# Counting pairs of nodes in one word: the first layer of a two-layer graph network on one core

## The reference

```python
def L0(edge_index, x):                       # the first layer: the change is here
    deg = segment_sum(ones, col)
    norm = deg_inv_sqrt[row] * deg_inv_sqrt[col]
    return segment_sum(x[row] * norm[:, None], col)

x = layernorm(x + L0(edge_index, x))
x = layernorm(x + L1(x, edge_index, edge_attr_4, edge_attr_32, W1, b1, W2, b2, si_w0, si_w1))
```

## Time and profile before

| | us |
|---|---|
| median of three runs | 3286.57 |
| profiled execution, its own time | 3279.85 |
| its span in the trace | 3278.0 |
| set-up, until the first gather | 82 |
| first layer, first gather to last table product | 82 to 1152 |
| second layer, from its first gather | 1171 to 3278 |

### The profile page before, as it was taken

The page is one execution under the profiler, slowest core; times in us unless marked ns, Lnnn a source line. Parts: engine busy times, 40 slices in busy tenths (PEclk is TensorE's granted clock), DMA queues, the critical chain, the costliest instruction groups (busy, mean ns, idle before and its releaser), DMA issues.

```text
span 3278.0 us, 48226 instructions
## 1 busy us (share of the span) xinstructions
PE 2556.6 (78%) x16782; PEld 1514.3 (46%) x16782; DVE 2876.8 (88%) x5078; ACT 1266.1 (39%) x1963; POOL 2400.0 (73%) x2477
## 2 busy tenths in 40 slices
PE   5798888898898867777777777777777777777776
PEld 4566666666676633333333333333343334333333
DVE  7787887787787759999999999999999999999998
ACT  2787887897888831111111111111111111111111
POOL 1777777777777757777777777777777777777775
PEclk7899999999999988998989999889889888888888
DMA  3111111111111121111111111111111111111112
GB/s 79 45 20 20 19 20 20 20 20 20 20 20 20 20 41 28 29 30 31 28 28 29 28 28 28 28 29 28 32 28 29 29 28 29 29 28 29 29 32 37
DMA packets 169490, 93.10 MB, mean 28 GB/s; under 512 B 112489, under 2 KB 155305, under 8 KB 169129
## 3 DMA queue, kind: packets, MB, share of 16 engines
q0 software_dynamic: 78336, 46.43, 10.6%
q1 hardware_dynamic: 90921, 43.61, 5.4%
HBM read 82.64 MB, written 7.22 MB: 27 GB/s over the span
## 4 chain that ended last, share of the span: by engine, by line
POOL 39%; DVE 23%; issue 17%; PE 14%; ACT 5%; DMA 1%; DVEq 1%; POOLq 0%; SPq 0%; ACTq 0%
POOL gathered L571 39%; DVE stage L1537 8%; PE ps L835 6%; PE ps L850 4%; DVE prod_all L1527 4%; ACT room L640 4%; DVE prod_all L1521 3%; DVE gathered L1209 2%; DVE stage L1511 1%; PE ps L775 1%; DVE stage L1507 1%; PE ps L742 1%; DVE prod_all L1343 1%; DMA gathered<-split_table,efT_all 1%; PE ps L822 1%
## 5 line engine op out<-in xcount | busy, mean ns | idle before, releaser
L571 POOL DMA_INDIRECT gathered<-x_table,idx x1664 | 1572.1, 945 | 533.0 <-issue 502.6
L571 POOL DMA_INDIRECT gathered<-split_table,efT_all x752 | 776.2, 1032 | 239.3 <-issue 232.9
L640 ACT ACTIVATE room<-ps 128x1089 bf16<-128x1089 f32 x800 | 877.7, 1206 | 181.1 <-PE ps L835 180.6
L955 PE MATMUL ps<-w2t,hT 128*128 128x512 f32 x1664 | 876.4, 653 | 16.3 <-ACT hT L691 16.2
L1537 DVE TENSOR_REDUCE stage<-prod_all 128x192 f32<-128x1536 f32 x416 | 725.3, 1744 | 3.2
L835 PE MATMUL ps<-prod_all,lane 128*128 128x363 bf16 x2640 | 571.1, 326 | 104.9 <-ACT room L640 54.5
L955 PEld LDWEIGHTS ps<-w2t,hT 128*128 128x128 f32 x1664 | 343.9, 213 | 373.3 <-issue 242.8
L943 PE MATMUL ps<-efT_all,w 128*128 128x512 f32 x416 | 270.2, 737 | 275.3 <-DMA sh<-in_sh 274.9
L850 PE MATMUL ps<-stage,room 128*128 128x96 bf16 x7840 | 474.4, 209 | 0.0
L850 PEld LDWEIGHTS ps<-stage,room 128*128 128x128 bf16 x7840 | 429.2, 100 | 82.5 <-issue 4.5
L699 ACT ACTIVATE stage<-gathered 128x64 f32<-128x64 f32 x416 | 105.1, 253 | 933.7 <-DMA gathered<-x_table,idx 933.7
(11 more groups left out here) (156 smaller groups left out, 1548.3 us busy)
## 6 DMA issues: line engine op xcount, KB each, us to landing
efT_all<-in_efT SPq DMA_DIRECT2D x104, 256.0 KB
gathered<-x_table,idx POOLq DMA_INDIRECT x1664, 2.4
gathered<-split_table,efT_all POOLq DMA_INDIRECT x752
sh<-in_sh SPq DMA_DIRECT2D x104, 32.0 KB
split_table<-stage SPq DMA_DIRECT2D x1, 2352.0 KB, 7.3
idx<-in_src SPq DMA_DIRECT2D x104, 8.0 KB, 1.6
scaled_x_table<-room SPq DMA_DIRECT2D x2, 784.0 KB, 3.4
x_table<-x_sb SPq DMA_DIRECT2D x7, 224.0 KB, 4.7
```

The source lines that it names most:

```text
L571: pool.indirect_dma_start(to, None, table, bass.IndirectOffsetOnAxis(ap=at, axis=0)).then_inc(landed, 16)
L640: act.activation(counts[u % 2][:, :, t * TWIN:(t + 1) * TWIN].rearrange("p (r h) w -> p r h w", r=RANGES), ps_ring[i % 2].rearrange("p r ( ...
L955: mm = pe.matmul(ps_bank[j % 2][v], hT[j // 2][:, t * P:(t + 1) * P], w2t[:].rearrange("p h c o i -> p (h c o i)"), start=False, stop=True)
```

## The change

Two neighbouring high parts h share one 32-bit word. The one-hot of the low part is no longer 1 but 1 or 65536, by the lowest bit of h, and `spread` is made of `11 (h/2) + target`: 550 columns instead of 1089. A count in PSUM is then `even + 65536 odd`; ACT writes it as an int32 word, and the two 16-bit halves of a word, read as fp16, are the two counts times 2^-24. `apply_counts` reads every second 16-bit element as its weights, and `take_rows` multiplies by 2^24. The ranges are two of 275 columns, two banks, and the ring has three entries in the same six banks. ACT copies all tiles; DVE copies none. The shares are new: 7 chunks and 16 units in a pattern, thus 38 gathered chunks (608 gathers) and 96 counted units (1056 tiles). The set-up computes the weight and the key of the pair in five more steps. Some small tiles moved into the room of a larger one.

```diff
-UPP = 8
-DVE_TILES = (5,)
-CPP = 5
+UPP = 16
+CPP = 7
 UW = 104
 D3 = 96
-RANGES = 3
-HR = 33
+RANGES = 2
+HR = 25
+RING = 3
+HALF = 2.0 ** 16
+HALF_ULP = 2.0 ** -24
...
-        ones_at = sb("ones_at", [P, 2 * CHUNKS], BF16)
+        ones_at = prod_all[:, 0].rearrange("p t c i o -> p (t c i o)")[:, DT:DT + CHUNKS].bitcast(BF16)
...
-        near_lanes = sb("near_lanes", [P, LW], F16)
-        low_lanes = sb("low_lanes", [P, 3, 44], F16)
+        near_lanes = sb("near_lanes", [P, 2 * WIDE], F16)
...
+        pos = flat[:, 3 * WIDE + DT:3 * WIDE + DT + U]
+        low_lanes = flat[:, 3 * WIDE - 66:3 * WIDE].bitcast(F16).rearrange("p (a b) -> p a b", b=44)
...
+        weight = flat[:, 3 * WIDE:3 * WIDE + DT]
...
-        counts = [t[:].bitcast(BF16).rearrange("p (h w) -> p h w", w=P) for t in room]
+        pair_words = [t[:].rearrange("p (h w) -> p h w", w=P) for t in room]
+        counts_i = [t[:].bitcast(I32).rearrange("p (h w) -> p h w", w=P) for t in room]
+        counts = [t[:].bitcast(F16).rearrange("p (h w v) -> p h w v", w=P, v=2) for t in room]
+        pair = dsrc.bitcast(F32)
...
-        ps_ring = [ps[:, RANGES * b:RANGES * (b + 1), 0:RW] for b in range(2)]
+        ps_ring = [ps[:, RANGES * b:RANGES * (b + 1), 0:RW] for b in range(RING)]
...
-                    act.wait_ge(s_evict, act_evicts(UT * (u - 1)))
+                    act.wait_ge(s_evict, UT * (u - 1))
                     act.wait_ge(s_apply, u - 1)
-                act.activation(counts[u % 2][:, :, t * TWIN:(t + 1) * TWIN].rearrange("p (r h) w -> p r h w", r=RANGES),
-                               ps_ring[i % 2].rearrange("p r (h w) -> p r h w", w=TWIN),
+                act.activation(counts_i[u % 2][:, :, t * TWIN:(t + 1) * TWIN].rearrange("p (r h) w -> p r h w", r=RANGES),
+                               ps_ring[i % RING].rearrange("p r (h w) -> p r h w", w=TWIN),
                                ACT.Copy).then_inc(s_evict, 1)
...
-                act.activation(rows_u[:], ps_dense, ACT.Copy).then_inc(s_dsb, 1)
+                act.activation(rows_u[:], ps_dense, ACT.Copy, scale=1.0 / HALF_ULP).then_inc(s_dsb, 1)
...
-                    if t not in DVE_TILES:
-                        evict(u, t)
+                    evict(u, t)
...
-                if i >= 2:
-                    if (i - 2) % UT in DVE_TILES:
-                        pe.wait_ge(s_evict_d, dve_evicts(i - 1))
-                    else:
-                        pe.wait_ge(s_evict, act_evicts(i - 1))
+                if i >= RING:
+                    pe.wait_ge(s_evict, i - RING + 1)
                 for r in range(RANGES):
-                    mm = pe.matmul(ps_ring[i % 2][:, r, :], ohlow[:, i % LR, 0:P], spread[i % KR][:, r * RW:(r + 1) * RW],
+                    mm = pe.matmul(ps_ring[i % RING][:, r, :], ohlow[:, i % LR, 0:P], spread[i % KR][:, r * RW:(r + 1) * RW],
                                    start=True, stop=True)
...
-                    pe.wait_ge(s_evict, act_evicts(UT * (u + 1)))
-                    pe.wait_ge(s_evict_d, dve_evicts(UT * (u + 1)))
+                    pe.wait_ge(s_evict, UT * (u + 1))
...
-                    mm = pe.matmul(ps_dense, counts[u % 2][:, h, :], table[:, h, :], start=(h == 0), stop=(h == NP - 1))
+                    mm = pe.matmul(ps_dense, counts[u % 2][:, h // 2, :, h % 2], table[:, h, :], start=(h == 0), stop=(h == NP - 1))
...
-            dve.wait_ge(s_key, 5)
-            for to, of, offset in zip(counted_places(key), counted_places(high), counted_tiles(rel_tile)):
+            dve.tensor_scalar(weight[:].bitcast(I32), dsrc, 7, 1, ALU.logical_shift_right,
+                              ALU.bitwise_and).then_inc(s_key, 1)
+            dve.wait_ge(s_key, 6)
+            dve.tensor_scalar(key[:].bitcast(I32), dsrc, 8, None, ALU.logical_shift_right).then_inc(s_key, 1)
+            dve.tensor_copy(weight[:], weight[:].bitcast(I32)).then_inc(s_key, 1)
+            dve.wait_ge(s_key, 8)
+            dve.tensor_copy(pair, key[:].bitcast(I32)).then_inc(s_key, 1)
+            dve.tensor_scalar(weight[:], weight[:], HALF - 1.0, 1.0, ALU.mult, ALU.add).then_inc(s_key, 1)
+            dve.wait_ge(s_key, 9)
+            for to, of, offset in zip(counted_places(key), counted_places(pair), counted_tiles(rel_tile)):
...
-                dve.tensor_scalar(ohlow[:, i % LR, 0:P + 1], low_lanes[:, :, 0:43], low[:, i:i + 1], None,
-                                  ALU.is_equal).then_inc(s_ohlow, 1)
-                dve.tensor_scalar(spread[i % KR], near_lanes[:], key[:, i:i + 1], None, ALU.is_equal).then_inc(s_spread, 1)
-
-            def evict(u, t):
-                i = u * UT + t
-                dve.wait_ge(s_count, i + 1)
-                if u >= 2:
-                    dve.wait_ge(s_apply, u - 1)
-                dve.tensor_copy(counts[u % 2][:, :, t * TWIN:(t + 1) * TWIN].rearrange("p (r h) w -> p r h w", r=RANGES),
-                                ps_ring[i % 2].rearrange("p r (h w) -> p r h w", w=TWIN)).then_inc(s_evict_d, 1)
+                dve.tensor_scalar(ohlow[:, i % LR, 0:P + 1], low_lanes[:, :, 0:43], low[:, i:i + 1], weight[:, i:i + 1],
+                                  ALU.is_equal, ALU.mult).then_inc(s_ohlow, 1)
+                dve.tensor_scalar(spread[i % KR], near_lanes[:, 0:LW], key[:, i:i + 1], None, ALU.is_equal).then_inc(s_spread, 1)
...
-                        made = u * UT + t - (KR - 1)
-                        if 0 <= made < DT and made % UT in DVE_TILES:
-                            evict(made // UT, made % UT)
```

More of the change, by code:

```diff
@@ L76, in gnn_program @@
     RW = HR * TWIN
-    LW = -(-RANGES * RW // 4) * 4
+    WORDS = RANGES * HR
+    LW = -(-WORDS * TWIN // 4) * 4
     RISE = n_out / CHUNKS
@@ L85, in gnn_program @@
     assert CHUNKS % 2 == 0 and CHUNKS >= 8 and n_out + UW <= SUMW and NP % SPLITS == 0
-    assert NP % HB == 0 and (RANGES - 1) * HR < NP <= RANGES * HR and RW <= WIDE and CHUNKS % 4 == 0 and NP % GB == 0
-    assert CG * TPC + DT == TILES and CG % 2 == 1 and UT * TWIN <= P and DT % TPC == 0 and NP * TWIN <= 2048
-    def dve_evicts(i):
-        return len(DVE_TILES) * (i // UT) + sum(t < i % UT for t in DVE_TILES)
-    def act_evicts(i):
-        return i - dve_evicts(i)
+    assert NP % HB == 0 and NP % 2 == 0 and (RANGES - 1) * HR < NP // 2 <= WORDS and RW <= WIDE < LW and CHUNKS % 4 == 0 and NP % GB == 0
+    assert CG * TPC + DT == TILES and UT * TWIN <= P and DT % TPC == 0 and NP * TWIN <= 2048
     def chunk_tile(n):
@@ L166, in gnn_program @@
         x_sb = sb("x_sb", [P, NP, D])
-        CW = HR * RANGES * P // 2
+        CW = WORDS * P
         room = [sb(f"room{k}", [P, CW]) for k in range(2)]
@@ L267, in gnn_program @@
         unit_first = sb("unit_first", [1, U], I32)
-        pos = sb("pos", [P, U])
-        place_u = sb("place_u", [P, UW])
-        rows_u = sb("rows_u", [P, D3])
         parts = sb("parts", [P, D])
@@ L273, in gnn_program @@
         flat = prod_all[:].rearrange("p b t c i o -> p (b t c i o)")
+        pos = flat[:, 3 * WIDE + DT:3 * WIDE + DT + U]
+        low_lanes = flat[:, 3 * WIDE - 66:3 * WIDE].bitcast(F16).rearrange("p (a b) -> p a b", b=44)
+        assert KR * LW // 2 <= 3 * WIDE - 66
+        weight = flat[:, 3 * WIDE:3 * WIDE + DT]
+        assert KR * LW // 2 <= 3 * WIDE and DT <= 3 * WIDE
+        place_u = flat[:, 3 * WIDE + DT + U:3 * WIDE + DT + U + UW]
+        rows_u = flat[:, 3 * WIDE + DT + U + UW:3 * WIDE + DT + U + UW + D3]
         flat1 = prod_all[:, 1].rearrange("p t c i o -> p (t c i o)")
@@ L369, in gnn_program @@
         s_evict = sem("s_evict")
-        s_evict_d = sem("s_evict_d")
         s_apply = sem("s_apply")
@@ L892, in _ @@
             with pe.Else():
-                pe.wait_ge(s_key, 7)
+                pe.wait_ge(s_key, 12)
                 pe.wait_ge(s_pos, 1)
@@ L903, in _ @@
                 pe.sem_inc(s_pace, QUARTERS * (CG - 2))
-                pe.wait_ge(s_evict, act_evicts(DT))
+                pe.wait_ge(s_evict, DT)
                 pe.wait_ge(s_dsb, U)
@@ L1029, in _ @@
             dve.tensor_copy(near_lanes[:, 0:WIDE], lane_f[:]).then_inc(s_dve_c, 1)
-            dve.tensor_scalar(near_lanes[:, WIDE:2 * WIDE], lane_f[:], float(WIDE), None, ALU.add).then_inc(s_dve_c, 1)
-            dve.tensor_scalar(near_lanes[:, 2 * WIDE:LW], lane_f[:, 0:LW - 2 * WIDE], 2.0 * WIDE, None,
+            dve.tensor_scalar(near_lanes[:, WIDE:LW], lane_f[:, 0:LW - WIDE], float(WIDE), None,
                               ALU.add).then_inc(s_dve_c, 1)
             dve.tensor_copy(low_lanes[:, :, 0:43], lane_f[:, 0:P + 1].rearrange("p (a b) -> p a b", b=43)).then_inc(s_dve_c, 1)
-            steps[0] += 4
+            steps[0] += 3
             slope = z_row[:].rearrange("p g f -> p (g f)")[:, 0:CHUNKS]
@@ L1391, in clear_pads @@
             def clear_pads(k):
-                dve.memset(counts[k][:, :, UT * TWIN:P], 0.0).then_inc(s_pads, 1)
+                dve.memset(pair_words[k][:, :, UT * TWIN:P], 0.0).then_inc(s_pads, 1)
```

(4 more changed lines are left out.)

## The result

The changed kernel takes **3032.2 us** (median of four runs, 3029.95 to 3034.41) against 3283.71 in the same session: ratio **0.9236**, 95% interval 0.9224 to 0.9248. The profiled execution has 3029.95 us, against 3076 forecast on that footing; its span is 3027.1.

What follows compares the result with a forecast made beforehand. Gathering on POOL bounds the kernel before; after the change PE's counting would: start at 108 us plus 96 units x 8.75 = 948 instead of 1152, gain 204, 3279.85 - 204 = 3076 us; range 3042 to 3150.

Steps and rivals of the forecast that it cites:

- ten products take 0.51, or 51 ns each: PE, counted half of the first layer: a product costs 51 ns, so a unit's 98 products take 5.0 us.
- POOL changes from bound to second: First layer: gathering alone ends at 914 us, PE's last product at 948, so POOL waits for PE's pace.
- rival 1: First layer: POOL stays the bound, PE's unit 8.4 us, layer ends at 922, gain 230, 3050 us; chance 0.13.
- a border at no cost: PE between two units: the forecast added 0.15 us for the wait on ACT's reading; the POOL-bound case assumed no border.
- its tightest engine: Counting in the kernel before: slack of some 8%, ACT tightest, copying at 1.09 us into a two-entry ring.
- Set-up: DVE's key instructions before the first gather: 6.5 us more (range 4.7 to 8.5), first gather at 89 us.
- the lower price: Five new key instructions on DVE: 0.60 us per 880 columns, 3.6 us in all; at the upper price, 1.24, 7.4 us.
- the two bounds: ACT's copy of 550 columns: 0.70 us by the straight line, 0.55 by the pitch.
- L742's row: PE matmul whose moving operand steps 32 bytes: its price would make a product 116 ns; the forecast kept 51 ns.
- DVE's tile: DVE's two one-hots per counted tile: 0.48 us, plus 0.05 for the second scalar and operation; a unit's tiles 5.8 us.
- Rivals 2 to 4: DVE becomes bound, 3196 us, 0.09; weights with gaps load slowly, 3686, or count not lightened, 3417, together 0.06.
- the unit on PE: PE per counted unit: 8.75 us, spread 8.5 to 9.3; every 0.1 us there is 9.6 us of time.

## Why the prediction went wrong

**The step that failed** is "ten products take 0.51, or 51 ns each". It was read as PE's own price, from a stretch in which PE waited for the ring that ACT empties. The changed kernel, and the old one with lighter copies, show 42 ns. 98 x 9 ns = 0.9 us a unit takes 8.75 to 7.85; measured by itself a unit is 7.2 + 0.34 + 0.27 = 7.8. The crossing with gathering stood at (914 - 108) / 96 = 8.4 in the forecast's own numbers. So this one term chose the wrong bound: "POOL changes from bound to second" is refuted, and rival 1, with a chance of 0.13, happened. It did not come for the reason that it gave, a border at no cost: the border cost 0.3 us, and the products made the unit short. The warning stood in the same part: the prediction itself named ACT as "its tightest engine" and PE's wait for it, 43.8 us, and yet counted the spacing of those very rows as products.

**The rest of the way, from rival 1's 922 to 900.89**, is three sizes. Without them rival 1's 3050 us would have held, which the range contains; it is the gathers above all that put the time below it. Gathers: 608 x 1.331 instead of 1.357, 16 us; the prediction held the pace of one gather fixed, though DVE works beside it. Set-up: the first gather at 85.38 instead of 89, 3.6 us. The timelines of POOL and DVE show why:

```profile
68.59 1.79 POOL L570 TENSOR_TENSOR efT_all<-efT_all,gathered 128x608 int32<-128x608 int32 x1
...
68.99 1.96 DVE L1140 CAST gathered<-key 128x1056 f32<-128x1056 int32 x1
70.87 0.70 DVE L1141 TENSOR_SCALAR prod_all<-prod_all 128x1056 int32<-128x1056 int32 x1
71.60 0.71 DVE L1144 TENSOR_SCALAR key<-prod_all 128x1056 int32<-128x1056 int32 x1
```

The five new instructions take 0.70 us each, close to the lower price (0.60 for 880 columns); long ones are those that ran while POOL did its index arithmetic, which ended at 70.38. With the keys behind the table all nine instructions of 1056 columns took 0.70 or 0.71. The third is what follows the last gather until the last product, 6.5 instead of 8 us.

**Right by their own steps:** 176 gathers as the largest part of the gain (238.8 us); the count at 0.24 us; ACT's copy of int32 words at 0.66, between the two bounds; the weights with a step at no extra price, where the choice went against L742's row; the second layer unchanged. DVE's tile was 0.52 against 0.48 + 0.05. Rivals 2 to 4 did not come: PE waited for DVE's one-hots 2.3 us and its weight loads 3.6 us in all, no product was near 73 ns, and ACT's copy was lightened. DVE had little slack, though: it was busy 598 us of 650.

**The range** was built around the unit on PE (3050 to 3130), and gave rival 1's own spread no room below: its gathers were taken as 1.357 us sharp.

## What to carry to other kernels

The spacing of two rows on an engine is that engine's price only if nothing released it late: look for the shortest spacing of the same rows, or for a stretch in which the engine that empties its buffers was idle. When two halves of a kernel end within some per cent of each other, the one shown as bound keeps its place unless the other's price is read free of waits; give both orders a chance that fits the distance between them. And the pace of the bound may itself depend on what the others do beside it, so it gets a spread like any other term.

## What the runs showed of the hardware

- Gathers of 0.94 us become 0.99 to 1.10 us in the mean, by what DVE does on its tiles. Two gathers that ran beside DVE instructions of 3.4 us, at the start of the first layer, took 3.6 and 4.1 us and ended 0.8 us after them; that a gather waits for such an instruction to end is a reading of these rows that no run settles; cutting long instructions up gained nothing.
- Cutting a one-hot of 1092 columns (pitch 0.41 us) into 552 and 540 takes 0.54 us and lengthens the gathers as well.
- A second scalar with a second operation on the low one-hot takes its pitch from 0.19 to 0.25 us.
- A weight load of 128 columns with its product of 96 takes 42 ns (granted clock 1.00, the level of 2.4 GHz) with elements 2 or 4 bytes apart, some 60 ns at 16 or 32 bytes (one run and two runs).
- DVE's integer operations and casts of 1056 columns take 0.70 us, and up to 1.96 us while POOL computes elementwise on integers.
